# One of four state groups of a selective scan: the scan writes SBUF, GpSimd multiplies by C

## The reference

```
dA  = exp(dt[..., None] * A)                       # 16 states for each of 384 channels
dBu = dt[..., None] * Bm[:, :, None, :] * u[..., None]
def step(h, inp):
    dA_t, dBu_t, C_t = inp
    h = dA_t * h + dBu_t
    y = jnp.einsum('bdn,bn->bd', h, C_t)           # multiply by C, sum over the 16 states
    return (h, y)
_, ys = jax.lax.scan(step, h0, (dA, dBu, Cm))
y = ys + u * Dp
y = y * silu(z)
```

## Time and profile before

| | |
|---|---|
| median of 3 runs | 1962.69 us (1962.38 to 1964.44) |
| the profiled execution | 1964.64 us, its span 1962.8 us |
| Mamba part | about the first 1400 us of the span |
| VectorE, TensorE, GpSimd, ScalarE busy over the span | 71%, 80%, 55%, 44% |

### The profile page before, as it was taken

One profiled execution on the slowest core, in us unless ns is written; L12 is line 12 of the kernel. 1 busy time (PEld: TensorE's weight loads), 2 busy tenths in 40 slices (PEclk: granted clock), 3 DMA queues, 4 the chain that ended last, 5 costly groups with the idle time before them and its releaser, 6 DMA issues. The chain is left out here.

```text
span 1962.8 us, 20242 instructions
## 1 busy us (share of the span) xinstructions
PE 1562.2 (80%) x5098; PEld 902.7 (46%) x5099; DVE 1384.7 (71%) x1552; ACT 868.8 (44%) x1944; POOL 1087.0 (55%) x635
## 2 busy tenths in 40 slices
PE   5867787896788688677868868886725999999997
PEld 3434344454445344344534434442413566666665
DVE  4499989998998998999899899989771122222221
ACT  2565545654555564465556456564301222222221
POOL 2466677676767768576775867667401233333332
PEclk8889889897998899899989989998857999999999
DMA  3412303131240413124031212312038111111111
GB/s 83 154 34 97 121 34 141 39 117 55 87 145 9 140 49 106 54 87 147 9 139 49 106 54 87 129 42 100 1 85 228 26 25 25 25 25 25 25 25 21
DMA packets 49163, 144.57 MB, mean 74 GB/s; under 512 B 13118, under 2 KB 26028, under 8 KB 48332
## 3 DMA queue, kind: packets, MB, share of 16 engines
q1 hardware_dynamic: 36956, 129.61, 19.6%
q0 software_dynamic: 12144, 14.30, 4.4%
HBM read 132.67 MB, written 11.21 MB: 73 GB/s over the span
## 5 line engine op out<-in xcount | busy, mean ns | idle before, releaser
L634 POOL TENSOR_TENSOR ring<-dtu,brep 128x1536 f32<-128x1536 f32 x192 | 666.6, 3474 | 377.9 <-DVE states L645 338.0
L657 PE MATMUL py<-ring,ident 128*128 128x384 f32 x1536 | 613.6, 545 | 222.6 <-ACT yg L670 141.2
L645 DVE TENSOR_TENSOR_SCAN states<-states,ring 128x768 f32<-128x768 f32 x384 | 674.3, 1756 | 91.9 <-ACT states L621 76.5
L657 PEld LDWEIGHTS py<-ring,ident 128*128 128x128 f32 x1536 | 306.6, 209 | 499.1 <-issue 155.5
L621 ACT ACTIVATE states<-dt_,aneg 128x376 f32<-128x376 f32 x768 | 405.8, 559 | 0.1
L647 DVE TENSOR_TENSOR ring<-states,crep 128x768 f32<-128x768 f32 x384 | 367.5, 957 | 13.2
L1304 PE MATMUL gu<-w,xsT 96*128 x660 | 299.1, 603 | 7.1 <-issue 6.5
L618 ACT ACTIVATE states<-zero_cols 128x16 f32<-128x16 f32 x384 | 70.0, 182 | 511.8 <-DVE ring L647 506.5
L1285 POOL DMA_INDIRECT xs<-x_scratch,yidx x56 | 55.3, 987 | 246.9 <-PE xps L1291 124.8
L1304 PEld LDWEIGHTS gu<-w,xsT 96*128 96x128 f32 x660 | 123.0, 193 | 146.0 <-issue 146.0
L1345 DVE COPY yidx<-place 128x1 int32 (+1 forms) x56 | 8.4, 153 | 253.3 <-DMA out_tokens<-ys,yidx 253.3
(11 more groups left out here) (225 smaller groups left out, 1457.8 us busy)
## 6 DMA issues: line engine op xcount, KB each, us to landing
brep<-b_c_rows SPq DMA_DIRECT2D x64, 768.0 KB, 4.1
crep<-b_c_rows SPq DMA_DIRECT2D x64, 768.0 KB, 5.9
w<-in_w SPq DMA_DIRECT2D x8, 1152.0 KB, 13.8
wd<-in_wd SPq DMA_DIRECT2D x8, 576.0 KB, 14.8
ptok<-in_p_tok SPq DMA_DIRECT2D x8, 384.0 KB, 3.7
pT<-in_p_T SPq DMA_DIRECT2D x8, 384.0 KB, 5.0
out_tokens<-h SPq DMA_DIRECT2D x8, 288.0 KB, 2.1
x_scratch<-x SPq DMA_DIRECT2D x8, 288.0 KB, 2.8
```

The costliest lines, as they stand in the source:

```text
L634: gp.tensor_tensor(ring[:, w % NRING], dtu[:, d, o, :].unsqueeze(1).to_broadcast([128, GN, T]), brep[:, ng], ALU.mult).then_inc(dbu_ok, 1)
L645: v.tensor_tensor_scan(h_in, h_in, x_in, 0.0, ALU.mult, ALU.add).then_inc(scan_ok, 1)
L657: mm = pe.matmul(py[:, 0:T], ident[:], ring[:, w % NRING, i, :], start=(ng == 0 and i == 0), stop=False)
```

## The change

In the units with ng = 3 the scan writes h into the slot of `ring`, over its own input, instead of into `states`, and VectorE goes on to the next scan. GpSimd multiplies the slot by `crep`, in two halves, at its own new step "scan", which stands behind "ahead" in the list. A new semaphore `hp_ok` is raised once for both halves. TensorE's sum of such a unit waits for it before its first matmul. ScalarE's decays of the unit that follows wait for the scan alone, since h no longer lies in `states`. The counts of the other products are renumbered.

```
 def sp_spread(...):
-            last_use = UD * (e - 1) + UD - NG + ng + 1
+            last_use = UD * (e - 1) + UD - NG + ng
             if which == "B":
-                wait(sp, dbu_ok, last_use)
+                wait(sp, dbu_ok, last_use + 1)
+            elif ng == NG - 1:
+                wait(sp, hp_ok, NC * e)
             else:
-                wait(sp, hc_ok, 2 * last_use)
+                wait(sp, hc_ok, 2 * (NG - 1) * NC * (e - 1) + 2 * (NG - 1) * (NC - 1) + 2 * ng + 2)
...
+        def products(c, w, i):
+            return 2 * (NG - 1) * 2 * NC * c + 2 * (NG - 1) * (w // NG) + 2 * (w % NG) + i + 1
+
+        def free_of(act, c, w, i):
+            at, v = (c, w - 1) if w else (c - 1, U2 - 1)
+            if v % NG == NG - 1:
+                wait(act, scan_ok, 2 * (U2 * at + v) + i + 1)
+            else:
+                wait(act, hc_ok, products(at, v, i))
...
 def act_decay(...):
             for i in range(2):
-                H = 2 * (U2 * c + w) + i
-                wait(act, hc_ok, H - 1)
+                free_of(act, c, w, i)
...
 def dve_scan(...):
                 v.wait_ge(da_ok, 2 * U + i + 1)
+                if ng == NG - 1:
+                    v.tensor_tensor_scan(x_in, h_in, x_in, 0.0, ALU.mult, ALU.add).then_inc(scan_ok, 1)
+                    continue
                 v.tensor_tensor_scan(h_in, h_in, x_in, 0.0, ALU.mult, ALU.add).then_inc(scan_ok, 1)
...
+        def pool_product(gp, c, w):
+            d, o, ng = unit(w)
+            if ng < NG - 1:
+                return
+            U = U2 * c + w
+            gp.wait_ge(crep_in[ng], 16 * (2 * c + d + 1))
+            for i in range(2):
+                x = half_of(ring[:, w % NRING], i)
+                gp.wait_ge(scan_ok, 2 * U + i + 1)
+                op = gp.tensor_tensor(x, x, half_of(crep[:, ng], i), ALU.mult)
+            op.then_inc(hp_ok, 1)
...
 def pe_sum(...):
             for i in range(GN):
-                if i % HALF == 0:
-                    pe.wait_ge(hc_ok, 2 * U + i // HALF + 1)
+                if ng == NG - 1:
+                    pe.wait_ge(hp_ok, NC * e + o + 1)
+                elif i % HALF == 0:
+                    pe.wait_ge(hc_ok, products(c, w, i // HALF))
...
-                "ahead": pool_input,
+                "ahead": pool_input, "scan": pool_product,
```

More of the change, by code:

```diff
@@ L191, in build_mamba @@
         hc_ok = sem("hc_ready")
+        hp_ok = sem("hc_ready_pool")
         y_ok = sem("states_summed")
```

## The result

The changed kernel takes 2099.31 us (median of 4 runs, 2098.18 to 2099.89) against 1962.63 us for the kernel before on the same chip: 1.0694 times as long, 95% interval 1.0675 to 1.0712. The forecast was 2068 us, with a range from 2000 to 2105. The sign and the range held, the time 6 us from the range's upper end; the sum of 106 us was 31 us too small.

What follows compares the result with a forecast made beforehand. VectorE looked like the bound, but with a second chain through ScalarE's decays and TensorE, ScalarE having 0.16 us of slack. 44 + 20 + 22 + 10 + 6.6 + 1.4 + 2 = 106 us on 1962.69 gave 2068 us, range 2000 to 2105.

Steps and rivals of the forecast that it cites:

- A: Unit 11 to 15, seven times: late pair and slow sum delay TensorE's chain and unit 15; +6.5 us six times, +44 in all.
- B: Unit 23 to unit 3 of the next chunk: same late chain, GpSimd on time; seven boundaries, +20 us.
- C: Unit 15 to 18, seven times: late sum and skip delay ScalarE's y copy and unit 18; +3.1 us each, +22.
- D: Unit 19 to 21, seven times: saving becomes a wait, time steps collide with GpSimd; +1.4 us each, +10.
- E: Unit 7: 1.77 us won, but GpSimd's next item moves onto the time steps, one collision +2.94; sum +6.6 us.
- F: Unit 3: 1.77 us won, but in five of seven chunks the argument reduction's third instruction collides, +3.11; sum +1.4 us.
- rest of chunk 7: Chunk 7 beyond unit 3 has no front work: nothing gained, 2 us for the later last sum.
- The saving: 48 group-3 units lose two VectorE products each, 1.77 us a unit, 85 us of VectorE time.
- Rival 1: The 85 us saved on VectorE arrive, each late sum falling into a gap of ScalarE: 1878 us; 4%.
- Rival 2: Slower by the chain alone: TensorE's clock stays up and no collision gets worse, +23, 1986 us; 20%, everything up to 2030.
- Rival 4: GpSimd becomes the bound, 119.4 us a chunk growing to 141; its waits take back the saving, 1963 us; 2%.
- rival 3: Everything waits: sums of 5.48 us (+20), short embedding instructions held up by a whole product (+17): 2105 us; 8%.

Runs made afterwards that it cites:

- e1: Changed kernel with GpSimd's pair of products ahead of its multiply for two units ahead, no longer behind it: 2028.82 us, 1.0344 of the kernel before.
- e5: Changed kernel with GpSimd's signal raised after each of its two products and TensorE's sum waiting for the halves one by one: 2061.00 us, 1.0499.
- e7: Changed kernel with the edits of e1 and e5 together, the pair ahead of the next input and a signal per half: 2001.01 us, 1.0198.
- e2: Changed kernel with GpSimd's two products cut to 8 of their 768 elements, still behind the multiply for two units ahead: 1963.87 us, 1.0012.
- e3: Kernel before, VectorE keeping all products, plus two same-size GpSimd multiplies that nobody waits for, at the changed kernel's place: 2018.25 us, 1.0289.
- e9: Changed kernel with GpSimd's pair replaced by five 8-element products and four memsets of 660 elements, as long and as late: 2097.37 us, 1.0690.
- e10: Kernel before with GpSimd multiplying by C only in units 4 and 16 of each chunk: 1936.27 us, 0.9862.
- e6: Changed kernel with 18 matmuls into unread columns of the sum's PSUM tile ahead of TensorE's wait for GpSimd: 2092.99 us, 1.0669.

## Why the prediction was right, and 31 us short

The working by stretch, with the measured extra summed over the chunks that the forecast counts (135 us from the first scan of the Mamba part to the first of its last unit, and in the spans too):

| term | forecast | measured |
|---|---|---|
| A, chunks 0 to 6 | +44 | +43.7 |
| B, seven boundaries | +20 | +26.7 |
| C, chunks 0 to 6 | +22 | +24.6 |
| D, chunks 0 to 6 | +10 | +8.5 |
| E, all chunks | +6.6 | +22.7 |
| F, all chunks | +1.4 | +8.9 |
| rest of chunk 7 | +2 | +0.7 |
| units 0 to 3 of chunk 0 | 0 | -1.1 |
| sum | +106 | +135 |

**Right: the chain behind a late sum, and A and D.** Each late sum pushes the decays one for one: in the loop the first scan of unit 15 follows 15.9 us behind the end of unit 11's skip matmul in the changed kernel (938.56 to 954.47), and as much in e1, e5 and e7, which make the sum earlier in steps. A goes with it from +45.7 over all chunks to 34.4 (e5), 21.1 (e1) and -1.6 (e7). Before the change the distance was 17.2 us (680.39 to 697.55 in the earlier trace rows), so about 1.2 us of lateness were free. The 0.16 us of the earlier trace rows, which the prediction calls decisive, is only ScalarE's room ahead of one decay; the forecast of A doesn't use it, since it goes by TensorE's order. That A came out to 0.3 us is in part luck: the sum took 5.4 to 5.5 us in chunks 0 and 1 and 4.3 to 4.4 in the others, so chunks 0 and 1 lost 6.6 and 7.2 us (forecast 5.4 and 6.5) and the others 5.9 to 6.0 (forecast 6.5). The durations taken from the nearest rows held: GpSimd's product has a median of 1814 ns where the line through the earlier trace rows gave 1.81 us, and the scan into SBUF takes 1740 ns where no change was taken. The saving was taken too small, 1.77 us a unit for 2.02. Rival 1, that the saving arrives, fell: even with a pair of 0.38 us (e2) it didn't. Rival 2, a clock that stays up and no worse collisions, fell by the slow sums and by E and F. Rival 4 fell as well: in the chunk of the table (850.50 to 1038.25) GpSimd is busy 141.9 of 187.8 us, the 141 that were forecast.

**Mis-sized: E, by 16 us.** The step was "One collision: +2.94 - 1.77 = +1.2". I had set aside in rival 3 that the short embedding instructions would wait out a whole product, because the longest of them beside GpSimd's norms took 0.63 us. That row was the wrong neighbour: a norm is another instruction than a two-input multiply. They did wait (3.84 us for the two of 0.83), in e3 too with a pair that feeds nobody, and not beside memsets in e9. The time steps then cost 0.66, not 2.94. Of rival 3 this half came true, 16 us for its 17. That the time lies near its 2105 us is in part chance: its other half, 20 us for slower sums, came to about 9, and it doesn't hold the error in F. In chunk 0, where I had counted 1.8 us won, it was 2.5 lost.

**Mis-sized: F, by 7.5 us.** The step was "the third ran free ... with the pair now beside it, 3.11 us more". In chunks 3 to 6 the number came out, +1.2 to +1.5 against +1.34, but by luck. VectorE, then GpSimd, behind unit 3 of the chunk of the table; the first row is from the trace before, the second answers to the second of the earlier trace rows, and the fourth is that of chunk 0:

```profile
617.17 0.63 DVE L366 TENSOR_SCALAR resid<-resid 128x384 f32<-128x384 f32 x2
```

```profile
861.83 2.44 DVE L363 SCALAR_TENSOR_TENSOR resid<-turns,resid 128x768 f32<-128x768 f32 x1
864.30 2.11 DVE L367 TENSOR_SCALAR resid<-resid 128x384 f32<-128x384 f32 x2
```

```profile
115.49 3.72 DVE L367 TENSOR_SCALAR resid<-resid 128x384 f32<-128x384 f32 x2
```

```profile
860.95 4.98 POOL L676 TENSOR_TENSOR ring<-ring,crep 128x768 f32<-128x768 f32 x2
```

The third instruction took 1.48 us more (from 0.96), not 3.11. The two short ones behind it, which I had not listed since they have one input, took 1.48 more as well (from 0.63), and the first of the reduction 0.5 to 0.9 more, since VectorE, ahead by the saving, began it 0.4 us behind the start of GpSimd's input and not 1.2. The collision also made the pair itself longer. The 7.5 us come from the other chunks. In chunk 0 (+3.8 against +1.34) the third took 4.05 us and the two short ones 3.72; in chunks 1 and 2 (-0.8 and -0.4 against -1.77) the short ones were held too; and in chunk 7 (+0.8 against -1.77) VectorE waited 2.14 us at L735 for TensorE's `pq`.

**Mis-sized: B and C, by 9 us: the slow sum.** I took 4.5 us for it (B's 17.1 us hold it). At unit 23 it took 5.49 us, the upper end in the earlier trace rows, with a slow skip matmul too; the third row is the sum of unit 15, in C:

```profile
828.11 5.49 PE L689 MATMUL py<-ring,ident 128*128 128x384 f32 x8 [5.83 <-POOL ring L676]
833.39 1.19 PE L692 MATMUL py<-u,skip_diag 128*128 128x384 f32 x2
...
963.33 4.79 PE L689 MATMUL py<-ring,ident 128*128 128x384 f32 x8 [5.83 <-POOL ring L676]
```

1.0 + 0.4 us more at seven boundaries is the difference in B (9.8 at most, 6.7 measured). In C it took 4.79 us: 0.3 more at seven places, 2.1 of the 2.6 by which C was short. The pause before it was 5.83 us in both cases, so the length of a pause alone doesn't fix the price; 4.3 to 5.5 us is what these runs show.

**The decomposition.** The saving of 97 us and the loss of 135 mean 232 us of cost. Collisions are 75 us of VectorE's busy time in the changed kernel; e3 measures 49 us of them and 56 us of run time with an idle pair of the same size. The rest, some 157 us, is put down to the lateness of the sums and to saving that turned into other waits; no run measures it by itself. Of it the place behind the input is worth 70 us (e1) and the common signal 38 (e5), both together 98 (e7). The parts are not independent (e9), and no finer split is claimed.

## What to carry to other kernels

Before work is moved to an idle engine, ask who waits for its result and what stands ahead of it in that engine's row: a pair that took 0.38 us gained nothing, in the largest stretch because it stood behind an item of 3.4 us and its sum came late. Take the piece whose consumer has room: two units won 1.4%, one whose sum waits for a copy anyway and one with 5.4 us until ScalarE needs what follows; six chosen by their place in a group lost 6.9%. And where two engines hold each other up, the price of a fuller row is paid by whatever instruction meets it, long or short, so list all of them and not the long ones only.

## What the runs showed of the hardware

- A VectorE instruction of 0.42 us with two SBUF inputs waited out a whole multiply of GpSimd: 3.84 us for two (0.83 before), ending with GpSimd's pair of 3.80 us. One-input TENSOR_SCALARs were held as well: 3.87 us against 0.76 for 1152 elements (e9), 5.35 against 0.63 for two of 384 (e7).
- The holding went both ways: GpSimd's pair took 4.98 us instead of 3.58 (e10) beside VectorE instructions of 2.44 and 2.11 us. Scans and products of VectorE, which have one of their inputs in PSUM, kept 1755 and 957 ns.
- A scan of 768 elements took 1740 ns into SBUF and 1755 into PSUM. Two scans into SBUF and the start of what follows took 3.31 us.
- TensorE's sum of 2.8 us took 4.3 to 5.5 us behind pauses of 4.2 us and more, with a granted clock of 0.66 in the one looked at. Behind shorter pauses it was either: at full speed behind 1.6 us (e6) and 3.05 us (e7), slow behind 3.08 us in the earlier trace rows. So the pause just ahead doesn't tell it alone.
